# The causal mask added by VectorE instead of TensorE, and steps of the pair loop reordered, in a fused three-layer kernel

## What is computed

```python
x = x + xattn(layernorm(x), ctx)     # fake_quant both to 0..255 codes, then matmul per batch
x = x + attn(layernorm(x), ...)      # qkv = h @ qkv_w + b; rope; 32 heads of 32; causal softmax; @ out_w + out_b
x = x + ffn(layernorm(x), ...)       # x @ W.T + bias + sum over 16 rank-16 updates
```

## Time and profile before

| | us |
|---|---|
| median of 3 runs (643.23 to 645.53) | 643.64 |
| the profiled execution | 645.53 |
| its span, first to last instruction | 643.9 |
| TensorE matmuls busy | 604.1 |
| VectorE busy | 448.6 |
| ScalarE busy | 297.6 |

### The profile page before, as it was taken

One profiled execution on the slowest core, in us unless ns is written; L12 is line 12 of the kernel. 1 busy time (PEld: TensorE's weight loads), 2 busy tenths in 40 slices (PEclk: granted clock), 3 DMA queues, 4 the chain that ended last, 5 costly groups with the idle time before them and its releaser, 6 DMA issues.

```text
span 643.9 us, 12627 instructions
## 1 busy us (share of the span) xinstructions
PE 604.1 (94%) x4832; PEld 299.6 (47%) x4832; DVE 448.6 (70%) x897; ACT 297.6 (46%) x374; POOL 11.1 (2%) x20
## 2 busy tenths in 40 slices
PE   1669987999999999999999999999999999899997
PEld 0234442454545555554445455544544554354453
DVE  7599995779747854885586568537865569767661
ACT  5888765774455545545634554555331233101010
POOL 3000000000000000000000000000000000000000
PEclk9879999999999999999999999999999999899999
DMA  9999896862284156317712751463240062023221
GB/s 320 385 388 383 331 301 235 280 227 70 98 263 164 67 195 213 115 65 259 258 69 84 251 186 65 168 219 103 98 163 2 1 212 97 35 78 119 84 79 49
DMA packets 38878, 109.17 MB, mean 170 GB/s; under 512 B 4026, under 2 KB 4282, under 8 KB 38848
## 3 DMA queue, kind: packets, MB, share of 16 engines
q1 hardware_dynamic: 37072, 104.35, 46.3%
q0 software_dynamic: 1344, 4.23, 1.7%
q10 hardware_dynamic: 432, 0.18, 0.1%
HBM read 100.35 MB, written 8.39 MB: 169 GB/s over the span
## 4 chain that ended last, share of the span: by engine, by line
PE 81%; DVE 11%; DMA 3%; SPq 2%; ACT 1%; issue 1%; DVEq 0%; ACTq 0%
PE dense L1104 16%; PE dense L1106 15%; PE dense L1105 15%; PE cross L1141 7%; PE turn L1095 6%; DVE wq L774 4%; PE dense L1235 4%; PE dense L1236 4%; PE dense L1237 4%; PE score L1198 2%; SPq L532 2%; DMA wq<-in_ctx 2%; PE score L1222 2%; DMA lnt<-in_ctx 1%; PE dense L1117 1%
## 5 line engine op out<-in xcount | busy, mean ns | idle before, releaser
L1104 PE MATMUL dense<-wq,xn_h 128*128 128x512 f16 x400 | 152.4, 381 | 0.0
L1105 PE MATMUL dense<-wq,xn_h 128*128 128x512 f16 x400 | 151.9, 380 | 0.0
L1106 PE MATMUL dense<-wq,xn_l 128*128 128x512 f16 x400 | 151.9, 380 | 0.0
L318 ACT ACTIVATE code<-raw,cst,qc 128x1024 uint8<-128x1024 f32 x74 | 90.2, 1237 | 17.9 <-DMA raw<-in_ctx 17.1
L1141 PE MATMUL cross<-code,q1t 128*128 128x512 f16 x256 | 74.7, 393 | 8.5 <-ACT code L318 4.2
L1106 PEld LDWEIGHTS dense<-wq,xn_l 128*128 128x128 f16 x400 | 39.2, 98 | 47.5 <-issue 0.6
L1104 PEld LDWEIGHTS dense<-wq,xn_h 128*128 128x128 f16 x400 | 39.2, 98 | 40.8 <-issue 2.8
L1105 PEld LDWEIGHTS dense<-wq,xn_h 128*128 128x128 f16 x400 | 39.3, 98 | 37.8 <-issue 0.9
L334 ACT ACTIVATE at<-turn 128x512 f32<-128x512 f32 x32 | 19.1, 597 | 76.8 <-PE turn L1095 76.0
L318 ACT ACTIVATE code<-lnt,cst,qc 128x1024 uint8<-128x1024 f32 x34 | 42.1, 1238 | 26.9 <-DMA lnt<-in_ctx 19.9
L803 DVE TENSOR_REDUCE smx<-score 128x8 f32<-128x512 f32 x32 | 22.0, 686 | 44.0 <-PE score L1198 44.0
(11 more groups left out here) (159 smaller groups left out, 935.8 us busy)
## 6 DMA issues: line engine op xcount, KB each, us to landing
raw<-in_ctx SPq DMA_DIRECT2D x74, 512.0 KB, 4.8
lnt<-in_ctx SPq DMA_DIRECT2D x34, 512.0 KB, 4.3
wo<-in_ctx SPq DMA_DIRECT2D x12, 512.0 KB, 9.1
wo<-in_qkv_w SPq DMA_DIRECT2D x12, 512.0 KB, 12.3
wq<-in_ctx SPq DMA_DIRECT2D x8, 512.0 KB, 11.5
wq<-in_qkv_w SPq DMA_DIRECT2D x8, 512.0 KB, 12.1
x_scratch<-xb SPq DMA_DIRECT2D x8, 512.0 KB, 3.2
wq<-x_scratch SPq DMA_DIRECT2D x8, 512.0 KB, 3.7
```

The source lines that it names most:

```text
L318: act.activation(low_bytes, src, ACT.Identity, scale=qc[:, 1:2], bias=z2).then_inc(s_u8, 1)
L1104: pe.matmul(bank[:, :], a_h[:, k, :], w_hi, start=(k == 0 and not started), stop=False)
L1105: pe.matmul(bank[:, :], a_h[:, k, :], w_lo, start=False, stop=False)
L1106: ins = pe.matmul(bank[:, :], a_l[:, k, :], w_hi, start=False, stop=(k == KC - 1 and not last))
```

## The change

`masked_by_vector(i)` is true for every pair from 1 on. There the two mask matmuls of each `scores` go, and `softmax_in` begins with a `scalar_tensor_tensor` that reads mask and scores and writes their sum to `pr`; maximum and subtraction then read `pr`. Waits that asked whether the softmax had read a bank of scores now ask for this instruction's semaphore. VectorE's `row_stats` moves from the middle of pair i - 1 to the beginning of pair i (still for pair i + 1, loop pairs 2 to 6), ahead of `row_codes`, and `rotate(i, 2)` comes between `softmax_in` 0 and 1. On TensorE the code turns move from block 0's k-step 5 to block 1's k-step 1, chunks 0 to 3 move later, `p_turn` 0 and 1 move from the end of block 3 to block 4, and the second scores from block 5's k-step 0 to block 4's k-step 6. On ScalarE `q(5)` moves ahead of the code evacuations and `q(6)` behind `qk_evac(i, 0)`. Pair 0 is unchanged.

```diff
--- before.py
+++ after.py
@@ -191,6 +191,7 @@
         s_v = sem("s_v")
         s_sc = sem("s_sc")
         s_sub = sem("s_sub")
+        s_msk = sem("s_msk")
         s_exp = sem("s_exp")
         s_p = sem("s_p")
         s_pt = sem("s_pt")
@@ -225,6 +226,10 @@
         block = es.enter_context(nc.Block())
         bias_stage = rope[:, 2:4, :].rearrange("p a n -> p (a n)")
         bias_low_stage = rope[:, 1, :].bitcast(F16)
+
+        def masked_by_vector(i):
+
+            return not isinstance(i, int) or i > 0
 
         def above(value):
 
@@ -428,14 +433,13 @@
                     if late:
                         weight_hi(j)
                 w(25)
-                q(2, 3, 4)
+                q(2, 3, 4, 5)
                 a_high(i + 1, 0)
                 a_high(i + 1, 1)
                 w(26)
-                q(5, 6)
                 w(27)
                 qk_evac(i, 0)
-                q(7, 8)
+                q(6, 7, 8)
                 w(28)
                 qk_evac(i, 1)
                 q(9)
@@ -800,8 +804,13 @@
                 p3 = pr[:, g % 2, :].rearrange("p (h k) -> p h k", k=SEQ)
                 s3 = S[g % 2][:, :].rearrange("p (h k) -> p h k", k=SEQ)
                 dve.wait_ge(s_sc, 4 * i + g + 1)
+                if masked_by_vector(i):
+                    dve.wait_ge(s_pt, 4 * i + g - 1)
+                    dve.scalar_tensor_tensor(p3, mask_rows, MASK_SEL, s3, ALU.mult, ALU.add).then_inc(s_msk, 1)
+                    dve.wait_ge(s_msk, 4 * i + g - 3)
+                    s3 = p3
                 link(dve.tensor_reduce(smx[:, g % 2, :], s3, AX.X, ALU.max))
-                if above(4 * i + g - 1):
+                if above(4 * i + g - 1) and not masked_by_vector(i):
                     dve.wait_ge(s_pt, 4 * i + g - 1)
                 dve.tensor_tensor(p3, s3, smx[:, g % 2, :].unsqueeze(2).to_broadcast([P, HPG, SEQ]),
                                   ALU.subtract).then_inc(s_sub, 1)
@@ -889,10 +898,12 @@
                 w(24, 25)
                 out_evac(0, 1)
 
-            def next_pair(i, more, late=False):
+            def next_pair(i, late=False):
                 def w(j):
                     if late:
                         weight_lo(j)
+                if not late:
+                    row_stats(i + 1, x_early)
                 row_codes(i + 1, x_early)
                 w(25)
                 rotate(i, 0)
@@ -904,15 +915,13 @@
                 w(28)
                 w(29)
                 softmax_in(i, 0)
+                rotate(i, 2)
                 softmax_in(i, 1)
-                rotate(i, 2)
                 softmax_out(i, 0)
                 softmax_out(i, 1)
                 w(30)
                 rotate(i, 3)
                 cross_evac(i + 1, 0)
-                if more:
-                    row_stats(i + 2, x_early)
                 softmax_in(i, 2)
                 softmax_in(i, 3)
                 w(31)
@@ -993,15 +1002,15 @@
 
             def run(i):
                 links["base"], links["n"] = start + per_pair * (i - 2), 0
-                next_pair(i, True)
+                next_pair(i)
                 assert links["n"] == per_pair, links["n"]
             first_pair()
-            next_pair(1, True, True)
+            next_pair(1, True)
             start = links["n"]
             with dve.Fori(2, PAIRS - 2) as i:
                 run(i)
             links["base"], links["n"] = start + per_pair * (PAIRS - 4), 0
-            next_pair(PAIRS - 2, False)
+            next_pair(PAIRS - 2)
             last_pair(PAIRS - 1)
 
             def stats3(s, k):
@@ -1178,17 +1187,26 @@
                 for e in range(2):
                     a_turn(i, e)
 
+            def read_by_softmax(i, count):
+
+                if masked_by_vector(i):
+                    pe.wait_ge(s_msk, 4 * i - 4 + count)
+                else:
+                    pe.wait_ge(s_sub, 4 * i + count)
+
             def scores(i, half):
 
                 done = 3 + half if isinstance(i, int) and i == 0 else 2 * half + 2
                 pe.wait_ge(s_qke, 4 * i + done)
                 if half:
-                    pe.wait_ge(s_sub, 4 * i + 2)
+                    read_by_softmax(i, 2)
                 elif above(4 * i):
                     pe.wait_ge(s_cl, 4 * i)
-                for n in range(2):
-                    rows = slice(n * SEQ, (n + 1) * SEQ)
-                    pe.matmul(S[n][:, :], row_of[rows, :], mask_rows[rows, :, :], start=True, stop=False)
+                vector = masked_by_vector(i)
+                if not vector:
+                    for n in range(2):
+                        rows = slice(n * SEQ, (n + 1) * SEQ)
+                        pe.matmul(S[n][:, :], row_of[rows, :], mask_rows[rows, :, :], start=True, stop=False)
                 for m in range(4):
                     for b in range(2):
                         c, col = m * P + b * SEQ, (2 * m + b) * SEQ
@@ -1196,7 +1214,7 @@
                             n, par = g // 2, g % 2
                             rows = slice(32 * g, 32 * g + 32)
                             ins = pe.matmul(S[n][par * SEQ:(par + 1) * SEQ, col:col + SEQ], qkt[rows, 2 * half, c:c + SEQ],
-                                            qkt[rows, 2 * half + 1, c:c + SEQ], start=False, stop=(m == 3 and b == 1))
+                                            qkt[rows, 2 * half + 1, c:c + SEQ], start=vector, stop=vector or (m == 3 and b == 1))
                             if m == 3 and b == 1 and par:
                                 ins.then_inc(s_sc, 1)
 
@@ -1210,7 +1228,7 @@
                 if half:
                     pe.wait_ge(s_cl, 4 * i + 2)
                 else:
-                    pe.wait_ge(s_sub, 4 * i + 4)
+                    read_by_softmax(i, 4)
 
             def values(i, half):
 
@@ -1386,17 +1404,21 @@
                     if not ahead:
                         merge(u)
 
+                def codes():
+                    if ahead:
+                        next_codes(i + 1)
+
                 def codes_turned(e):
                     if ahead:
                         pe.wait_ge(s_ah, 2 * i + 3 + e)
 
                 pe.wait_ge(s_xl, 2 * i + 2)
-                qkv(i, 0, {5: [at(next_codes, i + 1)]} if ahead else {})
-                qkv(i, 1, {0: [at(c, 0)], 2: [at(c, 1)], 4: [at(codes_turned, 0), at(qk_turn, i, 0)], 5: [at(c, 2), at(m, 0)], 7: [at(c, 3)]})
-                qkv(i, 2, {1: [at(c, 4)], 3: [at(codes_turned, 1), at(qk_turn, i, 1)], 4: [at(c, 5), at(m, 1)], 6: [at(scores, i, 0)], 7: [at(c, 6)]})
-                qkv(i, 3, {1: [at(c, 7)], 2: [at(m, 2)], 5: [at(turned, i, 0), at(qk_turn, i, 2)], 6: [at(turned, i, 2), at(p_turn, i, 0)], 7: [at(p_turn, i, 1)]})
-                qkv(i, 4, {1: [at(m, 3)], 4: [at(evacuated, i, 1), at(qk_turn, i, 3)], 6: [at(c, 8)], 7: [at(c, 9)]})
-                qkv(i, 5, {0: [at(scores, i, 1)], 1: [at(c, 10, 11), at(m, 4)], 2: [at(c, 12, 13), at(m, 5)], 3: [at(c, 14, 15), at(values_due, i, 0)], 4: [at(values, i, 0)],
+                qkv(i, 0)
+                qkv(i, 1, {1: [at(codes)], 4: [at(codes_turned, 0), at(qk_turn, i, 0)], 5: [at(c, 0), at(m, 0)], 6: [at(c, 1)], 7: [at(c, 2)]})
+                qkv(i, 2, {0: [at(c, 3)], 1: [at(c, 4)], 3: [at(codes_turned, 1), at(qk_turn, i, 1)], 4: [at(c, 5), at(m, 1)], 6: [at(scores, i, 0)], 7: [at(c, 6)]})
+                qkv(i, 3, {1: [at(c, 7)], 2: [at(m, 2)], 5: [at(turned, i, 0), at(qk_turn, i, 2)], })
+                qkv(i, 4, {0: [at(turned, i, 2), at(p_turn, i, 0)], 1: [at(m, 3)], 2: [at(p_turn, i, 1)], 4: [at(evacuated, i, 1), at(qk_turn, i, 3)], 6: [at(c, 8), at(scores, i, 1)], 7: [at(c, 9)]})
+                qkv(i, 5, {1: [at(c, 10, 11), at(m, 4)], 2: [at(c, 12, 13), at(m, 5)], 3: [at(c, 14, 15), at(values_due, i, 0)], 4: [at(values, i, 0)],
                            6: [at(evacuated, i, 0), at(p_turn, i, 2)], 7: [at(p_turn, i, 3)]})
                 project(i, 0, 0, {2: [at(values_due, i, 1)], 3: [at(values, i, 1)]})
                 project(i, 1, 0)
```

## The result

| us | before | after |
|---|---|---|
| median, runs side by side (6 and 6) | 644.74 | 648.53 |
| the profiled execution | 645.53 | 648.51 |
| its span | 643.9 | 646.8 |

The ratio is 1.0049, with a 95% interval from 1.0027 to 1.0070: **3.2 us slower**. The interval leaves out 1, so the change costs time; the size is just inside the 0.5% that the prediction calls the same, with an interval that reaches past it. The forecast was +0.9. In absolute numbers 648.53 lies 0.6 above the range's end of 647.9, but the kernel before itself took 1.1 more in the six runs here (644.74) than in the three that the prediction had (643.64); 1.0049 times 643.64 is 646.8, inside the range.

The account below looks back on a forecast made before the run. TensorE, busy 94% and without room inside a pair, was taken as the bound. Masks -4.5, old waits -1.4, new loop waits 5 x (0.40 + 0.42) and pair 1 +2.7 sum to +0.9: 643.64 becomes 644.5 us, range 639.0 to 647.9.

Parts of the forecast that it names:

- The masks' 0.32: TensorE, each scores step in pairs 1 to 7: dropping the mask matmuls saves 0.32 us, 14 times, -4.5 us.
- The old wait's seven times 0.20: TensorE, first turn of the probabilities, pairs 1 to 7: the existing 0.20 us wait is replaced, -1.4 us in all.
- The wait of the first `p_turn`: Middle of pairs 2 to 6: TensorE waits 0.42 us for ScalarE's `qk_evac(i, 2)`, which stands behind `q(13)`.
- rival 2: Slot chain of loads and chunks up to `q(12)` becomes the bound if loads are slow: 649 us, chance 0.13.
- rival 1: The new waits don't come while the masks' time does go: 639.5 us, chance 0.26.
- rival 3: The masks' time doesn't go, the scores' own start taking what the mask had covered: 647.6 us, chance 0.06.
- costs no TensorE time: Second scores' move: no loss, since `values_due` and its turns keep 2 us or more and `x_turn` keeps 0.4.
- At `qk_turn` 0 ... no further loss: Head of pairs 2 to 6: TensorE arrives at 9.68, `rotate` 0 is ready at 7.49 + 2.1 + 0.1, no further loss.
- The code turn's own wait: Head of pairs 2 to 6: TensorE waits 0.40 us at the code turns for VectorE's codes.
- Pair 1: 2.7 forecast: Pair 1, with split weight tiles passing between ScalarE and VectorE: 2.7 us of new waits, between 1.5 and 3.5.
- The wait of 2.2: Pair 1's middle: the usual 0.4 us wait plus a softmax 1.8 late, 2.2 us together.
- The maximum and the subtraction from SBUF: VectorE's softmax: reading SBUF instead of PSUM saves nothing; by the Trainium skill the forecast would be 1.6 us lower.

Follow-up runs that it names:

- e1: Kernel before without the mask matmuls from pair 1 on and nothing in their place: 641.93 us, ratio to before 0.9959.
- e9: Changed kernel, its orders untouched, without VectorE's mask instruction (no mask from pair 1 on): 642.99 us, ratio to before 0.9971.
- e10: Changed kernel with row statistics between the two `out_evac` of the pair before and `q(5)` behind the code evacuations: 643.07 us, ratio to before 0.9980.
- e4: Changed kernel with chunk 8 moved behind the second scores and chunk 9 to the next block: 646.41 us, ratio to before 1.0034.
- e3: Changed kernel with ScalarE's `qk_evac(i, 2)` ahead of `q(13)`: 648.74 us, ratio to before 1.0066.
- e5: Changed kernel with `qk_evac(i, 2)` ahead of `q(13)` and chunk 8 behind the second scores: 644.10 us, ratio to before 0.9987.
- e2: Changed kernel with row statistics moved from the pair's head to between the two `out_evac` of the pair before: 651.05 us, ratio to before 1.0115.
- e6: Changed kernel with e5's two edits and e10's two edits together: 640.58 us, ratio to before 0.9927.
- e7: e6 with pair 1 as in the kernel before (mask by TensorE, old order on all engines): 638.72 us, ratio to before 0.9905.
- e11: Changed kernel with pair 1's orders and masks as before, except statistics for pair 3 stay out of its middle: 644.20 us, ratio to before 0.9999.

## Why the prediction was right, and where it was not

**Right.** *The masks' 0.32*: the scores 0.31 behind the dense matmul, as foretold; 0.65 per pair in e1. *The old wait's seven times 0.20*: gone; pair 7 is 0.90 shorter, forecast 0.8. *The wait of the first `p_turn`*: forecast 0.42 behind `qk_evac(i, 2)`, measured 0.385 in five pairs. ScalarE's chain in pair 3 runs as it was added up, except that the evacuation right behind `q(13)` took 0.57 where 0.60 stood:

```profile
265.52 1.23 ACT L323 ACTIVATE code<-raw,cst,qc 128x1024 uint8<-128x1024 f32 x1
266.65 0.57 ACT L339 ACTIVATE at<-turn 128x512 f32<-128x512 f32 x1
```

*`q(12)`* starts at 261.48, P + 23.9 as forecast: the prediction's rival 2, the slot chain, did not come in the loop (in pair 1 of e9 and e10, not of after, `q(13)` did wait for its load, 2.31 and 0.80). Its rival 1 (no new waits) fell with the timeline above, its rival 3 (the masks' time stays) with e1.

**The step that failed most: chunk 8.** The prediction followed `softmax_in`, `rotate` and the bank of the queries' turn, and said of the second scores' move that it "costs no TensorE time"; it never asked what chunk 8, in the same slot, waits for. `cross_evac(i + 1, 0)` stands behind both softmaxes and `rotate(i, 3)`, so each mask instruction pushes it back by 0.72. VectorE, pair 3, kernel after the earlier trace rows:

```profile
258.78 0.69 DVE L809 SCALAR_TENSOR_TENSOR at<-c,score 128x512 f32<-128x512 f16 x1 [5.70 <-PE score L1216]
259.50 0.69 DVE L812 TENSOR_REDUCE smx<-at 128x8 f32<-128x512 f32 x1
260.22 0.69 DVE L815 TENSOR_TENSOR at<-at,smx 128x512 f32<-128x512 f32 x1
...
271.28 1.29 DVE L785 SCALAR_TENSOR_TENSOR xa<-cross,qc,xa 64x1024 f32<-64x1024 f32 x1
```

It ends at 272.57, and chunk 8 starts at 272.70 instead of 272.53. +0.84, missing from the sum; e4 takes it away alone, and pair 1's 0.66 with it.

**"At `qk_turn` 0 ... no further loss"** failed: 0.30 in each loop pair. The code turn's own wait was mis-sized the other way, 0.29 for 0.40 (in pair 6 0.17). Together 0.59 per pair where the sum had 0.40: +0.75 over pairs 2 to 6. Why `qk_turn` 0 waits in the loop and not in pair 6, which has the same order, is in VectorE's times. Pair 3 first:

```profile
242.55 0.81 DVE L727 TENSOR_SCALAR rope<-at,ab 128x1024 uint8<-128x1024 f32 x1
243.51 1.22 DVE L730 TENSOR_SCALAR_CACHE_REDUCE at<-rope 128x1024 f16<-128x1024 uint8 x1
...
244.78 0.27 DVE L732 TENSOR_SCALAR rs<-rs,qc 128x1 f32<-128x1 f32 x1
245.27 0.69 DVE L795 TENSOR_TENSOR rope<-dense,cst 128x512 f32<-128x512 f32 x1 [0.22 <-DVE rs L732]
```

and the same lines in pair 6, behind the loop:

```profile
422.24 0.81 DVE L727 TENSOR_SCALAR rope<-at,ab 128x1024 uint8<-128x1024 f32 x1
423.09 1.22 DVE L730 TENSOR_SCALAR_CACHE_REDUCE at<-rope 128x1024 f16<-128x1024 uint8 x1
...
424.35 0.27 DVE L732 TENSOR_SCALAR rs<-rs,qc 128x1 f32<-128x1 f32 x1
424.66 0.69 DVE L795 TENSOR_TENSOR rope<-dense,cst 128x512 f32<-128x512 f32 x1
```

0.96 against 0.85, 0.49 against 0.31, and once more 0.54 against 0.45 ahead of the rotation's last instruction (L801): 0.39 in all. The first of the three was in the prediction's sum, for the 2.23 of rows 8 comes from a loop pair of the kernel before. The other two were not: it put `rotate` 0 0.31 behind the start of the codes' last step and gave it 2.1, and in the loop these are 0.49 and 2.17. Those 0.25, and TensorE's coming 0.1 earlier since the code turn's wait was shorter, make the 0.30 but for a few hundredths.

**Pair 1: 2.7 forecast, 3.58 measured.** The wait of 2.2 split into 0.75 at `qk_turn` 1 and 1.63 at `p_turn` 0 (2.4), `rotate` 3 cost 0.54 for 0.5; what was missing is again chunk 8, 0.66. (The prediction's sign "pair 1 about 61.5" can't be held against the 60.64: it was reckoned from a pair of 59.6, of which 1.7 was the clock, as shown above.) The start of the softmax was forecast at P + 22.3 and came at 22.5, behind the last split tile:

```profile
136.56 1.23 DVE L778 SCALAR_TENSOR_TENSOR wo<-wo 128x1024 f16<-128x1024 f32 x1 [1.33 <-ACT wo L302]
137.70 0.68 DVE L809 SCALAR_TENSOR_TENSOR at<-c,score 128x512 f32<-128x512 f16 x1
```

So of the 2.3 us between forecast and result, 0.84 + 0.66 are chunk 8, 0.75 the pair's head, 0.2 the rest of pair 1, less 0.2 at `p_turn`. The verdict "the same" held, but not by the whole mechanism: nearly all the errors point one way and together are two and a half times the forecast, so that it stayed inside 0.5% is luck. The signs that it gave say so too: the period was to be 59.5 again and is 59.90.

**The maximum and the subtraction from SBUF.** The lines by form of the kernel after, then of the one before:

```profile
L815 DVE TENSOR_TENSOR at<-at,smx 128x512 f32<-128x512 f32 x28 | 19.4, 691 | 1.0
L812 DVE TENSOR_REDUCE smx<-at 128x8 f32<-128x512 f32 x28 | 19.2, 686 | 1.0
L809 DVE SCALAR_TENSOR_TENSOR at<-c,score 128x512 f32<-128x512 f16 x28 | 19.1, 683 | 45.1 <-PE score L1216 45.1
```

```profile
L806 DVE TENSOR_TENSOR at<-score,smx 128x512 f32<-128x512 f32 x32 | 22.1, 692 | 1.1
L803 DVE TENSOR_REDUCE smx<-score 128x8 f32<-128x512 f32 x32 | 22.0, 686 | 44.0 <-PE score L1198 44.0
```

686 and 686 ns, 692 and 691: the source makes no difference here, as the prediction took it from its rows. By the table of the Trainium skill (VectorE: DVE Perf Modes, "The TRN2 errata") it would be 65 ns less from SBUF, an estimate from 58 against 120 cycles; the trace does not agree, and the saving of 1.6 us that would follow did not come.

## What to carry to other kernels

When work is put into an engine's order, list every consumer behind it up to the next point where that engine has idle time, with each one's own deadline: the first late one is easily found, the second shows only when the first is mended (e3, e4, e5), and it may sit on another engine or a queue (e2). An instruction that moves should be judged with what is queued behind it on the DMA queue and behind that on the next engine. And the pair that differs (here pair 1, already limited by something else) is worth an order of its own: left as it was, with four orders mended in the others, the same change of masks gives 1% instead of costing half a percent.

## What was not expected of the hardware

**Waits in a loop.** The 0.11, 0.18 and 0.09 above recur in pairs 2 to 5, whose waits compare a semaphore with a register, and not in pair 6, whose waits compare with constants. The kernel before has the first and the last of them in the same way (0.96 against 0.84, 0.54 against 0.45). The register alone isn't enough of a reason: `rotate` 2 and 3 of the same loop pair have the same waits, and there the last instruction comes after 0.45 as in pair 6 (261.76 to 262.21). What it is stays open; no run took it apart.

**The clock after an idle time.** In pair 1 of e9 TensorE was idle for 2.8 us and then had 0.51 of full speed, the lower of its two levels, over 3.5 us:

```profile
145.99:148.81 2.82, 0.38 (x2) 0.00 (x0) 2.75 (x5) 1.72 (x2) 0.00 (x0) 1.00 0.28 113
148.81:152.27 3.46, 3.46 (x11) 1.83 (x11) 3.39 (x6) 0.60 (x1) 0.00 (x0) 0.51 0.00 1
```

In e10 the gap there was 2.29 and the clock fell too, 0.7 behind it; in the kernel after it was 1.85, and the clock stayed. But a gap alone doesn't decide: the tail has one of 2.61 in each of these kernels, and behind it the clock fell to the lower level in before, after, e1, e5 and e6 (the tail's next turns of `lnt` then come 25.0 us behind the last ones of pair 7) and did not in the other eight (23.3). The tail of e3:

```profile
550.33:552.94 2.61, 0.38 (x2) 0.00 (x1) 2.33 (x10) 0.02 (x1) 0.00 (x0) 1.00 0.01 2
552.94:556.40 3.46, 3.46 (x16) 1.58 (x17) 3.37 (x6) 1.87 (x3) 0.00 (x0) 1.00 0.00 0
```

That is 1.7 us between executions of the same stretch of code; a second such place lies between 103 and 116 us, where in e7 the fall came late enough to lengthen pair 1 to 60.80, against 58.19 in e11 with nearly the same pair 1 (53.54 and 53.82 from its first matmul on). Single profiles of this kernel can't be compared to better than some 2 us outside the loop, which is why the periods above are all taken inside it.
